# A six-layer macaron kernel: local stream's inverse norms by log, exp and a Newton step, and the distance attention's setup pipelined

## The reference

```python
x = x + 0.5 * gelu_ffn(layernorm(x))
x = x + distance_attention(layernorm(x))        # 16 heads of 8
x = x + 0.5 * gelu_ffn(layernorm(x))
x = x + 0.5 * local_layers(layernorm(x))        # 2 layers each
x = x + causal_attention(layernorm(x))          # 16 heads of 64
x = x + 0.5 * local_layers(layernorm(x))
```

```python
h = shift_token(x)
q, k, v = split(h @ wqkv)
q = q / clip(norm(q), 1e-12) * qs               # and k with ks
q, k = rotary_xpos(q, k)
x = x + local_attention(q * 8, k, v) @ wo
h = layernorm(shift_token(x)) * lg + lb
a, g = split(h @ w1 + b1)
x = x + (a * gelu(g)) @ w2 + b2
```

## Time and profile before

| what | value |
|---|---|
| median of 3 executions | 3575.77 us (3573.64 to 3576.94) |
| the profiled execution | 3580.72 us, span 3578.6 us |
| PE busy | 3183.2 us (89%) |
| ACT busy | 2167.5 us (61%) |
| DVE busy | 1976.4 us (55%) |
| POOL busy | 1737.4 us (49%) |
| L896, POOL, power of the squared norms | 128 times, 374.1 us |
| L889, POOL, cosine part + sine part | 128 times, 302.1 us |
| L850, POOL, rows times inverse norms | 128 times, 243.4 us |
| L857, POOL, probabilities times inverse totals | 128 times, 242.6 us |
| L1231, DVE, squares summed over heads | 128 times, 154.6 us |
| table loads at L1186 and L1201 | 32 times each, 41.1 us each |

### The profile page before, as it was taken

How to read it: one execution, slowest core, us unless ns; L and a number is a source line. 1 busy time by engine, 2 the same in 40 slices (tenths; PEclk the granted TensorE clock), 3 DMA queues, 4 the chain that set the end, 5 groups by cost and what they waited for, 6 DMA issues and landing times. The chain is left out here.

```text
span 3578.6 us, 73165 instructions
## 1 busy us (share of the span) xinstructions
PE 3183.2 (89%) x26564; PEld 1951.8 (55%) x26564; DVE 1976.4 (55%) x4014; ACT 2167.5 (61%) x3580; POOL 1737.4 (49%) x1412
## 2 busy tenths in 40 slices
PE   6499999868999999749999999999998599999995
PEld 5222222435666666526666666666665366666663
DVE  4200000337777777545556555656565577777773
ACT  2399999526666666535555555555554366666663
POOL 1100000039889988523333333333332698998882
PEclk9699999979999999979999999999999799999998
DMA  1122222021111111100000000000000211111111
GB/s 33 20 36 39 36 38 38 7 74 34 35 36 38 37 36 34 25 10 9 7 6 9 6 9 6 9 6 9 6 6 4 86 37 35 37 37 37 35 33 36
DMA packets 124405, 95.70 MB, mean 27 GB/s; under 512 B 80448, under 2 KB 100544, under 8 KB 123968
## 3 DMA queue, kind: packets, MB, share of 16 engines
q1 hardware_dynamic: 122784, 89.41, 11.4%
q10 hardware_dynamic: 1440, 3.80, 0.3%
HBM read 22.90 MB, written 2.10 MB: 7 GB/s over the span
## 5 line engine op out<-in xcount | busy, mean ns | idle before, releaser
L1761 POOL TENSOR_SCALAR e<-e,inv 128x768 f32<-128x768 f32 (+7 forms) x512 | 375.3, 746 | 761.8 <-DVE inv L1653 761.8
L1724 ACT ACTIVATE e<-e,nmax 128x768 f32<-128x768 f32 (+7 forms) x512 | 395.4, 772 | 429.5 <-DVE e L1648 426.2
L1648 DVE TENSOR_SCALAR_CACHE_REDUCE e<-slot 128x768 f32<-128x768 f32 (+7 forms) x512 | 376.2, 754 | 243.8 <-PE slot L1537 243.8
L530 ACT ACTIVATE e<-slot 128x1024 f32<-128x1024 f32 x512 | 472.9, 1091 | 43.8 <-PE slot L466 43.8
L896 POOL TENSOR_TENSOR inv_norm<-floored,minus_half 128x16 f32<-128x16 f32 x128 | 374.1, 2922 | 10.7
L1641 DVE COPY eT<-slot 128x512 f32<-128x512 f32 (+3 forms) x384 | 238.7, 622 | 234.1 <-PE slot L1548 233.9
L1548 PE MATMUL slot<-ident,e 128*128 128x128 f32 x2304 | 332.7, 280 | 8.7 <-POOL e L1761 3.7
L1531 PE MATMUL slot<-key,q 64*128 64x512 f32 (+3 forms) x1536 | 318.1, 518 | 19.0 <-ACT v L1711 12.7
L889 POOL TENSOR_TENSOR rot<-cosine,sine 128x1024 f32<-128x1024 f32 x128 | 302.1, 2360 | 44.3 <-DVE sine L1228 44.3
L857 POOL TENSOR_TENSOR prob<-prob,inv_total 128x1024 f32<-128x1024 f32 x128 | 242.6, 1895 | 129.2 <-DVE inv_total L1246 129.2
L1548 PEld LDWEIGHTS slot<-ident,e 128*128 128x128 f32 x2304 | 252.5, 141 | 92.0 <-issue 68.9
(11 more groups left out here) (161 smaller groups left out, 6420.8 us busy)
## 6 DMA issues: line engine op xcount, KB each, us to landing
v_mix<-v SPq DMA_DIRECT2D x256, 128.0 KB, 2.3
w_qkv<-in_causal_w_dram SPq DMA_DIRECT2D x32, 192.0 KB
query<-q_hi SPq DMA_DIRECT2D x128, 32.0 KB
keys<-q_hi SPq DMA_DIRECT2D x128, 32.0 KB
query<-q_lo SPq DMA_DIRECT2D x128, 32.0 KB
keys<-q_lo SPq DMA_DIRECT2D x128, 32.0 KB
hs<-H SPq DMA_DIRECT2D x32, 128.0 KB
h1s<-H SPq DMA_DIRECT2D x32, 128.0 KB
```

The source lines that it names most:

```text
L530: act.activation(e[n % E_RING][:], c.slots[n % RING][:].rearrange(flat), ACT.Exp, scale=2 * SCALE).then_inc(e_ready, 1)
L1648: dve.tensor_scalar(e[n % RING][h][:, 0:cols], c.slots[h][:].rearrange(flat)[:, 0:cols], -1.0, None, ALU.mult, ALU.min, accum_out=nmax[:, ...
L1724: act.activation(part, part, ACT.Exp, bias=nmax[:, n, h:h + 1], scale=-1.0, accum_out=total[:, n, h:h + 1]).then_inc(e_ready, 1)
L1761: pool.tensor_scalar(part, part, inv[:, n, h:h + 1], 1.0, ALU.mult, ALU.mult).then_inc(scaled, 1)
```

## The change

Four things change.

1. In the local layers the power on POOL is replaced. POOL still floors the squared norms (now before `rotated`, into a double buffer). ACT takes their logarithm and the exponential of minus half of it, in the slot after, between `attention_out` and `heads`. POOL then makes one Newton step of four small instructions (square, product, -0.5 and 1.5, product) ahead of `unit_rows`. The table that is preloaded for Exp is now asked for by the name of a set.
2. DVE sums the squares over heads ahead of the rotation, and ahead of its wait for POOL's `rotated`.
3. The bias b2 is no longer added by POOL. It is a row of w2 that belongs to an unused hidden unit, whose two biases (0.0625 and 16) make its value 1. Its two DMAs, and the waits for it, go.
4. In the distance attention the two setup blocks are one, in which normalising, transposing and projecting follow each other batch by batch; and the 40 DMAs that stack unit 0 are issued in that block, as the high parts, the low parts and the norms of batch 0 become ready.

The diff, cut to its core:

```diff
@@ distance_attention @@
+        def stack_head(sp, stacked, b, g, j):
...
-            normalised_columns(nc, c, xT, moments=False)
+            row_statistics(nc, c, moments=False)
             with nc.Block() as block:
+                @block.sync
+                def _(sp):
+                    heads = [stack_head(sp, stacked, 0, 0, j) for j in range(GROUP)]
+                    sp.wait_ge(cleared, 5)
+                    sp.wait_ge(hi_ready, 1)
+                    for high, _, _ in heads:
+                        high()
+                    sp.wait_ge(lo_ready, 1)
+                    for _, low, _ in heads:
+                        low()
+                    sp.wait_ge(norm_hi_ready, 1)
+                    sp.wait_ge(norm_lo_ready, 1)
+                    for _, _, norms in heads:
+                        norms()
...
@@ distance_attention, PE @@
+                    for b in range(B):
+                        columns(b)
+                        if b < B - 1:
+                            turn_rows(2 * b + 2)
+                            turn_rows(2 * b + 3)
+                        rows(b)
+                        norms(b)
...
@@ distance_attention, ACT @@
+                    columns(0)
+                    columns(1)
                     for b in range(B):
                         act.wait_ge(qT_ready, b + 1)
                         act.activation(q_hi[:, b * S:(b + 1) * S], c.slots[1][:].rearrange(flat), ACT.Copy).then_inc(hi_ready, 1)
                         if b >= 2:
                             act.wait_ge(norm_ready, b - 1)
                         act.activation(sq[b % 2][:], c.slots[1][:].rearrange(flat), ACT.Square).then_inc(sq_ready, 1)
+                        if b < B - 1:
+                            columns(2 * b + 2)
+                            columns(2 * b + 3)
+                        act.wait_ge(norm_ready, b + 1)
+                        act.activation(n_hl[0:HEADS, b * S:(b + 1) * S], c.slots[2][0:HEADS].rearrange(flat),
+                                       ACT.Copy).then_inc(norm_hi_ready, 1)
+                        act.wait_ge(q_ready, b + 1)
+                        act.activation(q_all[:, b * TPB:(b + 1) * TPB, :, :].rearrange("p t h d -> p (t h d)"),
+                                       c.slots[0][:].rearrange(flat), ACT.Copy).then_inc(q_out, 1)
@@ distance_attention, DVE @@
                     for b in range(B):
                         cols = slice(b * S, (b + 1) * S)
+                        if b < B - 1:
+                            rows(2 * b + 2)
+                            rows(2 * b + 3)
...
                         dve.tensor_tensor(q_lo[:, cols], c.slots[1][:].rearrange(flat), q_hi[:, cols].bitcast(F32),
                                           ALU.subtract).then_inc(lo_ready, 1)
+                        dve.wait_ge(norm_hi_ready, b + 1)
+                        dve.tensor_tensor(n_hl[32:32 + HEADS, cols], c.slots[2][0:HEADS].rearrange(flat),
+                                          n_hl[0:HEADS, cols].bitcast(F32), ALU.subtract).then_inc(norm_lo_ready, 1)
@@ local_layers, POOL @@
+                def inverse_norms(a):
+                    first = first_inv[:, a.j % 2, :]
+                    pool.wait_ge(first_inv_ready, a.t + 1)
...
+                    pool.tensor_tensor(inv_square[:], first, first, ALU.mult).then_inc(inv_square_ready, 1)
...
+                    pool.tensor_tensor(product[:], inv_square[:], floored[:, a.j % 2, :], ALU.mult).then_inc(correction_ready, 1)
...
+                    pool.tensor_scalar(correction[:], product[:], -0.5, 1.5, ALU.mult, ALU.add).then_inc(correction_ready, 1)
...
+                    pool.tensor_tensor(inv_norm[:, a.j % 2, :], correction[:], first, ALU.mult).then_inc(inv_norm_ready, 1)
...
                         if last := tile(step, r, 1, depth):
+                            inverse_norms(last)
                             unit_rows(last)
                         if r == 1 and (ffn := group(step, FFN, depth)):
                             deviations(ffn)
-                            add_b2(ffn)
                         if own := tile(step, r, 0, depth):
+                            floor_norms(own)
                             rotated(own)
-                            inverse_norms(own)
@@ local_layers, ACT @@
+                def inverse_norms(a):
+                    act.wait_ge(floor_ready, 3 * a.t + 3)
+                    act.activation(log_norm2[:], floored[:, a.j % 2, :], ACT.Ln).then_inc(log_norm2_ready, 1)
+                    act.wait_ge(log_norm2_ready, a.t + 1)
+                    if known(a.t, 2):
+                        act.wait_ge(inv_norm_ready, a.t - 1)
+                    act.activation(first_inv[:, a.j % 2, :], log_norm2[:], ACT.Exp, scale=-0.5).then_inc(first_inv_ready, 1)
...
                         if r < 3 and out:
                             attention_out(out)
+                        if last := tile(step, r, 1, depth):
+                            inverse_norms(last)
                         if scored:
                             heads(scored)
                         if r == 3 and ffn:
                             gates(ffn, 2)
-                            act.preload_act_table(ACT.Exp)
+                            act.preload_act_table_set("natural_log_exp_and_others")
@@ local_layers, DVE @@
                     dve.wait_ge(sq_ready, a.t + 1)
+                    if known(a.t, 2):
+                        dve.wait_ge(floor_ready, 3 * a.t - 3)
+                    dve.tensor_reduce(norm2[:, a.j % 2, :], sq[:].rearrange("p (h d) -> p h d", d=D), AX.X, ALU.add)\
+                       .then_inc(norm2_ready, 1)
                     if known(a.t, 1):
                         dve.wait_ge(rot_ready, a.t)
                     dve.tensor_tensor(cos4, qk, table(0, 0, D), ALU.mult)
...
-                    if known(a.t, 2):
-                        dve.wait_ge(inv_norm_ready, a.t - 1)
-                    dve.tensor_reduce(norm2[:, a.j % 2, :], sq[:].rearrange("p (h d) -> p h d", d=D), AX.X, ALU.add)\
-                       .then_inc(norm2_ready, 1)
```

More of the change, by code:

```diff
@@ L316, in _, with turn_rows, columns @@
                 def _(pe):
[L317 to L326, removed]
-                            m = pe.matmul(c.slots[2][0:HEADS, half, :], sel[:], sq[b % 2][:, half * 512:half * 512 + 512],
-                                          start=True, stop=True)
-                        m.then_inc(norm_ready, 1)
[L331 to L337, removed]
+                    def turn_rows(i):
+                        pe.wait_ge(xn_ready, G * (i + 1))
+                        if i >= 2:
+                            pe.wait_ge(columns_ready, i - 1)
+                        for j in range(G):
+                            m = pe.transpose(c.slots[3][:, i % 2, j * P:(j + 1) * P], xn[:, i % 2, j, :], c.ident[:])
+                        m.then_inc(turned, 1)
+                    def columns(b):
+                        pe.wait_ge(columns_ready, 2 * b + 2)
                         if b:
@@ L344, in _, with rows @@
                         m.then_inc(qT_ready, 1)
-                        if b == 0:
-                            pe.wait_ge(merged_ready, 1)
-                            pe.matmul(c.slots[3][:, 0, 0:P], merged[:], wo[:], start=True, stop=True).then_inc(eff_ready, 1)
-                        if b:
-                            norms(b - 1)
-                    norms(B - 1)
+                    def rows(b):
+                        if b:
+                            pe.wait_ge(q_out, b)
+                        for t in range(TPB):
+                            m = pe.matmul(c.slots[0][:, t // 4, (t % 4) * P:(t % 4 + 1) * P],
+                                          xT[:, (b * TPB + t) * P:(b * TPB + t + 1) * P], wk[:], start=True, stop=True)
+                        m.then_inc(q_ready, 1)
@@ new lines, in norms @@
+                    def norms(b):
+                        pe.wait_ge(sq_ready, b + 1)
+                        if b:
+                            pe.wait_ge(norm_hi_ready, b)
+                            pe.wait_ge(norm_lo_ready, b)
+                        else:
+                            pe.wait_ge(merged_ready, 1)
+                            pe.wait_ge(eff_out, 1)
+                        for half in range(2):
+                            m = pe.matmul(c.slots[2][0:HEADS, half, :], sel[:], sq[b % 2][:, half * 512:half * 512 + 512],
+                                          start=True, stop=True)
+                        m.then_inc(norm_ready, 1)
@@ L598, in distance_attention @@
             clear()
+        clear_stacked()
 def local_layers(nc, c, d, moments=True):
```

143 lines of the change are left out of this document (85 added, 58 removed).

## The result

The changed kernel took **3567.18 us** (median of 8 runs, 3559.48 to 3568.74) against 3575.26 us for the kernel before (8 runs, 3573.64 to 3580.58): a ratio of 0.997, 95% interval 0.9961 to 0.9979. That is 8.1 us or 0.3% faster.

A forecast was written before the change was run, and what follows sets the result against it. PE was taken to bound steady local steps, with POOL just behind, and POOL the fill. Setup -33.5, fills -11.6 and steps +27.4 gave -17.7: 3563 us profiled, 3558 as median, range 3500 to 3605.

The forecast's parts named there:

- Three unasked loads: Slot 3 on ACT: table loads for Ln, Exp and Gelu again, turning a step's -1.39 us into +1.16 in depth 0.
- Two loads: Rival for slot 3: Ln's load serves Exp too, -52.9 us in all, 3523 us; chance 0.14.
- none: Rival for slot 3: no extra loads on the path, -88.2 us in all, 3488 us; chance 0.10.
- Steady steps: Full local steps behind the fill: +1.16 us each in depth 0, +0.88 in depth 1, 27.4 us for two calls.
- the credit for POOL's waits: Slot 2 of a local step: PE's waits for residual and scaling shrink, 1.39 us in depth 0, 1.59 in depth 1.
- Fill: Local call, product 0 to slot 3 of step 2: 105.33 us shrinks to 97.9; with other terms -5.8 per call.
- The 0.9 for the two b2 DMAs: Start of a local call: dropping b2's two DMAs ahead of the first product saves 0.9 us.
- Setup: Distance attention: with merged blocks and early DMAs the first scores start at 133.7 instead of 167.26, -33.5 us.
- The circle: Distance setup, per batch: norms, their copy, low part, next rows, transposes, products and norms again, about 8.9 us.
- The clock's credit: Distance attention, unit 0's first exponentials: another -5.7 us should the clock stay up across the gap; not counted.
- The slower rival: Slot 3: the loads idle PE and its clock falls, some 1.8 us lost each, +50 us, 3608; chance 0.20.

The follow-up runs named there:

- order_moved: moved with the old order inside a tile (sum over heads behind the rotation, rotation ahead of the floor): 3508.36 us, ratio 0.9806.
- setup_only: The changed distance setup with the local stream of the kernel before: 3544.68 us, ratio 0.991 against the kernel before.
- rows_ahead: moved with POOL's memsets held until 16 tiles are normalised and DVE's next rows ahead of the norms' low part: 3491.06 us, ratio 0.9761.
- moved: The changed kernel with slot 3's Ln and Exp behind the third Gelu and the asked load: 3494.10 us, ratio 0.9775; once more 3492.98 us.
- the local half alone: The changed local stream with the distance setup of the kernel before: 3589.43 us, ratio 1.004 against the kernel before.
- pow_back: The changed kernel with POOL's power in place of Ln, Exp and Newton step; early sum, early floor and folded bias stay: 3503.01 us, ratio 0.9789.

## Why the prediction was right, and where it was not

The direction, the three loads and their price held. The part of the gain that is missing in the profiled executions comes mainly from the fill. That the forecast is no further off is in part luck: errors of 14.0 us one way stand against 8.3 the other (the sum at the end of this section).

- **Three unasked loads: right, in number and place.** Two loads (3523) and none (3488) were the rivals; both have now run as kernels of their own, at 3527 and 3494. Against the step without loads I gave them 2.55 us in depth 0 and 2.47 in depth 1; they cost 2.45 in both. The forecast set the Trainium skill's 1.38 us of drain per switch (ScalarE: Activation LUTs, What ACT_TABLE_LOAD costs) aside by the trace of before, and rightly: from 1170.90 the next instruction follows at 1172.20, 1.30 us for load and all. The same page's remark that Ln followed by Exp needs one load, as one set holds both, is not what this kernel got: 28 loads stand at each of the two.
- **Steady steps.** Forecast +1.16 and +0.88, measured +0.73 (44.85 against 44.12) and +0.85. What was too small is the credit for POOL's waits in depth 0: 1.39, measured 1.72 (44.12 against 42.40 without loads); 1.59 in depth 1, measured 1.6. My reading that the small operations give back in slot 1 what b2 frees, so that the cosine would wait as before without the early sum, is what `order_moved` shows. In all, the thirteen steps of a call cost 8.3 and 8.7 us, not 13.7. Some 3.4 of the difference is the 0.43 a step in the eight of depth 0; some 2.7 is that the clock no longer falls in two steps of a call, which I had not counted: those two take 45.7 us where they took 46.2. What I also did not see is that the bias alone gives 1.24 of the 1.72: the power, which I removed first in my sum, needed no removing, as it filled idle time in three slots of four.
- **Fill: the term that was mis-sized most.** I let it shrink by 7.4 us to the twelfth product; it shrank by 2.4 and 1.5. I took three slots of 8.0 and one of 6.6; they took 8.4 on the mean and 8.65; the six of 8.75 took 8.91, and the one of 14.8 took 15.4. Everything behind the twelfth product cost +11.6 and +12.4 against 16.2 forecast (13.7 for the steps, 2.5 for slot 3), though what follows the call's last own product has +3.3 and +3.7 of it: one more slot 3 with its loads, which is the 2.5, and a fall of the clock (below). The 0.9 for the two b2 DMAs ahead of the first product can't be told from the scatter: 32.2 here against 31.9 in `setup_only`, which still has them.
- **Setup: mis-sized by 6.** -33.5 forecast, -27.6 at the first scores. The loss lies in the first batch. The first q_hi came 2.6 us late (104.70, not 102.1), since DVE's rows ran beside the memsets at half their pace, and the first low part of the norms ended at 111.8, not 107: on PE the next tiles' transposes (1.40 us) and a product (1.95) stand ahead of the norms. The circle itself was right: from there to the last low part, which ended at 138.5 and not at 133, it took 26.7 us, three times the forecast's 8.9. Inside, it was not even: two rounds of 10.4 us, with PE waiting 1.6 and 0.4 us for rows and the clock falling (0.59 at 114 to 117, 0.64 at 126 to 129), and one of 5.9 us with no rows left to turn. That SP's 40 DMAs are not the bound was right for this kernel (they end at 132.6), and no longer in `rows_ahead`, where they begin behind the memsets. The clock's credit, which I did not count, came for 4.6 of 5.7. So the -32.2 at the first local product is near the -33.5 by luck: a term that was 6 too large, and one that was left out.
- **The slower rival** (the clock falls in slot 3) did not happen in the steps: PE idled 0.80 and 1.34 us there, and no step's clock fell. It did happen once a call, in the slot 3 behind the last own product, where PE idles a third time, 1.11 us for probT:

```profile
1449.00:1452.00 3.00, 1.24 (x16) 0.86 (x8) 2.45 (x4) 2.85 (x4) 2.92 (x3) 1.00 0.00 1
1452.00:1455.00 3.00, 2.41 (x35) 2.30 (x36) 1.88 (x2) 1.98 (x3) 0.42 (x1) 0.59 0.22 54
```

  It is low for 3.4 us there in both calls of the changed kernel, and at that place in neither call of `moved`. The rival's sign was nearer than its mechanism, as the local half alone is 15 us slower.

Summed, against the forecast of 3563 for the profiled execution: the setup lost 1.3 us by the time of the local call, the two fills 10.9 and b2's DMAs 1.8, and steps and drains won 8.3: 5.7 in all, and 3568.65 measured.

## What to carry to other kernels

A function that moves to ScalarE is to be priced with the tables that it turns over, and not by its own length alone: here 0.43 us of Ln and Exp brought 3.85 us of loads between two Gelus, and placing the same two instructions behind the load that is there anyway gave 72 us. Ask which slot of a saturated engine has no idle time before removing its longest operation: 1.28 us in slot 1 was worth 43 us of run time, 2.92 us four times a step 6 to 9, and with the old order nothing. When a block is merged to pipeline it, look at what used to run beside nothing; memsets that stood beside no rows in the kernel before doubled the time of the rows they now stood next to. And compare the clock of the two traces before putting a difference down to the order of the work: here it was worth 4 to 7 us in a setup, and 1.3 in a step.

## What the runs showed that I had not expected

- A ScalarE activation of 16 elements per partition takes 212 to 216 ns, and the GpSimd operations of the Newton step, of that size, 203 to 221 ns; the four take 1.30 us from the first to the unit rows behind them.
- VectorE's normalising of a 128x128 tile took 0.27 or 0.52 us, and one pair of tiles over 5 us, depending on how GpSimd's 128x1024 memsets (0.95 us) fell beside it.
- After a gap of some 3 us between two blocks TensorE's clock was at 0.50 for some 10 us in `moved` and some 24 in `pow_back`, whose code differs in nothing there.
